# A router's ranking from one table of differences, its masks merged, and the low rows rounded by ScalarE and TensorE

## The reference

```python
u_inner = u @ W_in.T + b_in;  x, z = split(u_inner)
dbc = x @ W_x.T + b_x                      # delta_raw, B, C
delta = softplus(delta_raw @ W_dt.T + b_dt)
h_t = h_{t-1} * exp(delta_t * A) + x_t * delta_t * B_t ;  y_t = sum_n h_t C_t
y = (y + x * D) * silu(z) ; x = x + y @ W_out.T + b_out

logits = xn @ Wg.T + bg ; scores = softmax(logits)        # 4 experts
topv, topi = top_k(scores, 2)
base = xn @ Wi.T ; low = xn @ A[e].T (4 ranks for each expert)
out = sum over the 2 chosen e of score_e * (relu(base + low_e @ B_e.T) @ Wo.T)
```

## Time and profile before

| | |
|---|---|
| median of 3 runs | 1856.04 us (1853.64 to 1858.43) |
| profiled execution | 1855.82 us, of which span 1854.0 us |
| granted TensorE clock, mean of the span | 0.959 of full speed |
| VectorE busy | 1763.7 us (95% of the span), 2060 instructions |
| GpSimd busy | 1714.5 us (92%) |
| TensorE busy | 1624.7 us (88%) |
| ScalarE busy | 1503.9 us (81%) |

### The profile page before, as it was taken

One profiled execution on the slowest core, in us unless ns is written; L12 is line 12 of the kernel. 1 busy time (PEld: TensorE's weight loads), 2 busy tenths in 40 slices (PEclk: granted clock), 3 DMA queues, 4 the chain that ended last, 5 costly groups with the idle time before them and its releaser, 6 DMA issues.

```text
span 1854.0 us, 26281 instructions
## 1 busy us (share of the span) xinstructions
PE 1624.7 (88%) x7052; PEld 830.2 (45%) x7052; DVE 1763.7 (95%) x2060; ACT 1503.9 (81%) x3113; POOL 1714.5 (92%) x649
## 2 busy tenths in 40 slices
PE   6657689998998999889898989989899998988999
PEld 3213244444444444444444444444444444444465
DVE  5999999999999999999999999999999999999951
ACT  4776889888898988889898888979888897988643
POOL 1999999999999999999999999999999999999910
PEclk9767799999999999999999999999999999999999
DMA  6655565655656565554747556574665657475200
GB/s 211 138 137 139 118 154 140 157 129 138 152 107 174 131 166 128 141 141 108 181 116 170 140 129 146 111 185 118 165 143 127 137 118 190 99 167 136 63 7 18
DMA packets 150070, 249.07 MB, mean 134 GB/s; under 512 B 22432, under 2 KB 47264, under 8 KB 149408
## 3 DMA queue, kind: packets, MB, share of 16 engines
q1 hardware_dynamic: 145456, 231.09, 51.0%
q0 software_dynamic: 4464, 16.25, 4.6%
HBM read 188.01 MB, written 42.99 MB: 125 GB/s over the span
## 4 chain that ended last, share of the span: by engine, by line
DVE 35%; PE 18%; issue 17%; POOL 16%; ACT 7%; DMA 2%; SPq 1%; DVEq 0%; POOLq 0%; ACTq 0%
DVE decay L1395 15%; POOL hs L1470 10%; DVE hs L1382 9%; DVE hs L1395 7%; POOL hs L1482 4%; PE bank L914 3%; PE bank L962 3%; ACT decay L1203 3%; PE y_ps L998 2%; PE bank L984 2%; POOL z_dt L1450 2%; PE bank L918 1%; DMA b_rep<-bc_scratch 1%; DVE silu L1282 1%; PE bank L979 1%
## 5 line engine op out<-in xcount | busy, mean ns | idle before, releaser
L1470 POOL TENSOR_TENSOR hs<-dx_rep,b_rep 128x2048 f32<-128x2048 f32 x255 | 1188.9, 4678 | 43.1 <-DVE hs L1411 40.0
L1395 DVE TENSOR_TENSOR_SCAN decay<-decay,state,hs 128x512 f32<-128x512 f32 x640 | 791.5, 1270 | 4.9 <-ACT decay L1203 3.9
L1203 ACT ACTIVATE decay<-dt_rep,a_sb 128x512 f32<-128x512 f32 x1024 | 692.5, 685 | 20.6 <-DVE dx_rep L1409 1.8
L1395 DVE TENSOR_TENSOR_SCAN hs<-decay,state,hs 128x512 f32<-128x512 f32 x384 | 485.8, 1265 | 1.3 <-ACT decay L1203 0.8
L1482 POOL TENSOR_TENSOR hs<-hs,c_rep 128x1024 f32<-128x1024 f32 x192 | 476.5, 2482 | 6.0 <-ACT state L1217 5.8
L1382 DVE TENSOR_TENSOR hs<-decay,c_rep 128x1024 f32<-128x1024 f32 x320 | 383.7, 1199 | 0.0
L998 PE MATMUL y_ps<-hs,nsum 128*32 128x512 f32 x2048 | 292.2, 645 | 53.5 <-POOL hs L1482 44.8
L914 PE MATMUL bank<-xn_t,w_in_sb 128*128 128x512 f32 x512 | 252.6, 622 | 10.3 <-DVE silu L1282 3.5
L962 PE MATMUL bank<-w_i_sb,x_t 128*128 128x512 f32 x492 | 249.6, 631 | 8.2 <-DVE silu L1282 6.9
L984 PE MATMUL bank<-w_o_sb,r_t 128*128 128x256 f32 x944 | 217.0, 383 | 4.7 <-ACT r_t L1186 2.7
L984 PEld LDWEIGHTS bank<-w_o_sb,r_t 128*128 128x128 f32 x944 | 178.8, 191 | 56.2 <-issue 28.5
(11 more groups left out here) (170 smaller groups left out, 1823.9 us busy)
## 6 DMA issues: line engine op xcount, KB each, us to landing
dx_rep<-rep_scratch SPq DMA_DIRECT2D x252, 256.0 KB, 4.7
dt_rep<-rep_scratch SPq DMA_DIRECT2D x252, 256.0 KB, 7.6
b_rep<-bc_scratch SPq DMA_DIRECT2D x256, 64.0 KB, 4.0
c_rep<-bc_scratch SPq DMA_DIRECT2D x256, 64.0 KB, 2.4
rep_scratch<-z_dt SPq DMA_DIRECT2D x64, 256.0 KB, 2.6
rep_scratch<-e_dt SPq DMA_DIRECT2D x64, 256.0 KB, 2.7
e_dt<-z_dt POOLq DMA_DIRECT2D x31, 512.0 KB, 4.6
xin<-in_u SPq DMA_DIRECT2D x16, 512.0 KB, 4.1
```

What stands on the lines that cost most here:

```text
L1203: nc.scalar.activation(decay[:, j, :], dt_rep[m % 2][:, j, :], ACT.Exp, scale=a_sb[:, J * s + j:J * s + j + 1]).then_inc(decay_ready, 1)
L1395: v.tensor_tensor_scan(hs[s % 4][:, j, :] if kept else decay[:, j, :], decay[:, j, :], hs[s % 4][:, j, :], state[:, b, n:n + 1], ALU.mult, ...
L1470: nc.gpsimd.tensor_tensor(hs[s % 4][:], dx_rep[m % 2][:], b_rep[:, k, :].unsqueeze(1).to_broadcast([P, J, T]), ALU.mult).then_inc(input_re ...
```

## The change

The routing takes seven parts instead of ten (`LAST_H` 6). One table `gap` holds all differences of logits, one `scalar_tensor_tensor` makes from it and `tri` the table of "stands ahead of" with ties settled, and its sum is the rank. One instruction makes both masks `sel` (rank 0 and rank 1), and one multiplies both into the low rows. The second copy of the logits, the tables, the rank and the masked rows no longer lie in PSUM: `lg`, `gap`, `gt`, `rank`, `sel` and `low` are SBUF tiles. The two writes of `pk` leave VectorE: ScalarE spreads `low` into `pk` four times (a new job H0 of ScalarE), and rounding and rest are made behind the transposes: ScalarE rounds the transposed rows into `low_t` (I0), TensorE subtracts from the same bank what was rounded, by a product with `neg_low` (I1), and ScalarE writes `low_t` again (I1). The tables of all engines are moved a little around that.

```diff
 DVE_SIDE
     "H3 post | H4 post | H5 post | H6 post",
-    "K2 late, H7 post | H8 post | H9 post | M0 post",
+    "K2 late |  |  | M0 post",
 ACT_SIDE
-    " | J7 late, S7 late | T6 late, X0 post | T7 late",
-    " | I0 post | E3 main | V3 main",
+    " | J7 late, S7 late | T6 late, X0 post, H0 post | T7 late",
+    " | I0 post, I1 post | E3 main | V3 main",
 ...
 # TensorE
+                if letter == "I" and i == 1:
+                    pe.wait_ge(low_hi, q + 1)
+                    pe.matmul(banks[used("I0", c, AHEAD[when])[0]][:], neg_low[:], low_t[:], start=False, stop=True,
+                              skip_group_check=True).then_inc(low_rest, 1)
+                    return
 ...
 # ScalarE
+                elif letter == "H":
+                    act.wait_ge(low_ready, q + 1)
+                    nc.scalar.copy(pk[:].rearrange("p t a b w -> p (t a) b w"),
+                                   low[:].rearrange("p t a w -> p (t a) w").unsqueeze(2).to_broadcast([P, 2 * TT, 4, NE * LR])
+                                   ).then_inc(freed[used("H0", c, AHEAD[when])[0]], 1)
+                elif letter == "I" and i == 1:
+                    act.wait_ge(low_rest, q + 1)
+                    b, _ = used("I0", c, AHEAD[when])
+                    nc.scalar.activation(low_t[:], banks[b][:], ACT.Identity).then_inc(freed[b], 1)
 ...
 # VectorE, route
                 if i == 0:
                     dve.wait_ge(filled[b], count)
-                    v.tensor_tensor(lg[:], z[:, :, 0:NE], b_g_sb[:], ALU.add)
-                    last = v.tensor_tensor(lgp, z[:, :, 0:NE], b_g_sb[:], ALU.add)
+                    last = v.tensor_tensor(lg[:], z[:, :, 0:NE], b_g_sb[:], ALU.add)
 ...
                     v.tensor_reduce(mx[:], lg[:], AX, ALU.max)
-                    v.tensor_tensor(gtp, lgp.unsqueeze(2).to_broadcast([P, TT, NE, NE]),
-                                    lg[:].unsqueeze(3).to_broadcast([P, TT, NE, NE]), ALU.is_gt)
-                    last = v.tensor_tensor(eqp, lgp.unsqueeze(2).to_broadcast([P, TT, NE, NE]),
-                                           lg[:].unsqueeze(3).to_broadcast([P, TT, NE, NE]), ALU.is_equal)
+                    last = v.tensor_tensor(gap[:], lg[:].unsqueeze(2).to_broadcast(grid), lg[:].unsqueeze(3).to_broadcast(grid),
+                                           ALU.subtract)
                 elif i == 2:
-                    v.tensor_tensor(lm[:, :, 0:NE], lgp, mx[:].unsqueeze(2).to_broadcast([P, TT, NE]), ALU.subtract)
-                    last = v.tensor_tensor(eq[:], eqp, tri[:], ALU.mult)
+                    v.tensor_tensor(lm[:, :, 0:NE], lg[:], mx[:].unsqueeze(2).to_broadcast([P, TT, NE]), ALU.subtract)
+                    last = v.scalar_tensor_tensor(out=gt[:], in0=tri[:], scalar=-TINY, in1=gap[:], op0=ALU.mult, op1=ALU.is_lt)
                 elif i == 3:
-                    last = v.tensor_tensor(gt[:], gtp, eq[:], ALU.add)
+                    last = v.tensor_reduce(rank[:], gt[:].rearrange("p t e f -> p (t e) f"), AX, ALU.add)
                 elif i == 4:
-                    last = v.tensor_reduce(rank, gt[:], AX, ALU.add)
+                    last = v.tensor_tensor(sel[:, 0::2], rank[:].unsqueeze(1).to_broadcast([P, 2, TT * NE]),
+                                           ranks[:].unsqueeze(2).to_broadcast([P, 2, TT * NE]), ALU.is_equal)
                 elif i == 5:
-                    for a in range(2):
-                        last = v.tensor_scalar(sel[:, a], rank, float(a), None, ALU.is_equal)
+                    v.tensor_tensor(own2[:], lm[:, :, 0:NE], sel[:, 2].rearrange("p (t e) -> p t e", t=TT), ALU.mult)
+                    last = v.tensor_tensor(sel[:, 1], sel[:, 2], sel[:, 0], ALU.subtract)
                 elif i == 6:
+                    v.tensor_reduce(lm[:, :, NE], own2[:], AX, ALU.add).then_inc(router, 1)
+                    shape = [P, 2, TT, NE, LR]
+                    last = v.tensor_tensor(
+                        low[:].rearrange("p t a (e r) -> p a t e r", e=NE),
+                        z[:, :, NE:].rearrange("p t (e r) -> p t e r", e=NE).unsqueeze(1).to_broadcast(shape),
+                        sel[:, 0:2].rearrange("p a (t e) -> p a t e", t=TT).unsqueeze(4).to_broadcast(shape), ALU.mult)
```

More of the change, by code:

```diff
@@ L42 @@
 BOUND = 41.0
+TINY = 1.1754944e-38
 PE_SIDE = [
@@ L415, in bank_jobs @@
                     name = {"Y": "F", "Z": "J"}.get(name[0], name[0]) + name[1]
-                if name[0] in BANK_JOBS and name != "C1":
+                if name[0] in BANK_JOBS and name not in ("C1", "I1"):
                     yield name, when, J * s + j
@@ L571, in block_program @@
         gt = sb("gt", [P, TT, NE, NE])
-        eq = sb("eq", [P, TT, NE, NE])
-        sel = sb("sel", [P, 2, TT, NE])
-        change = sb("change", [P, TT, NE])
+        gap = sb("gap", [P, TT, NE, NE])
+        rank = sb("rank", [P, TT * NE])
+        ranks = sb("ranks", [P, 2])
+        sel = sb("sel", [P, 3, TT * NE])
         own2 = sb("own2", [P, TT, NE])
         wgt = [sb(f"wgt{i}", [P, 2, TT]) for i in range(2)]
-        pk = sb("pk", [P, TT, 2, 2, 2, NE * LR])
+        low = sb("low", [P, TT, 2, NE * LR])
+        pk = sb("pk", [P, TT, 2, 4, NE * LR])
         decay = ctx.enter_context(nc.psum_tensor("decay", [P, J, T], F32))
@@ L950, in job_pe @@
                     for t in range(TT):
-                        mm = pe.transpose(ps[:, t * P:(t + 1) * P], pk[:, t].rearrange("p a b c d -> p (a b c d)"), ident[:])
+                        mm = pe.matmul(ps[:, t * P:(t + 1) * P], pk[:, t].rearrange("p a b w -> p (a b w)"), ident[:],
+                                       start=t == 0, stop=False, is_transpose=True, skip_group_check=True)
                 elif letter in "ZJ":
@@ L1227, in _ @@
                 v.memset(consts[:, n], value)
+            for rank_of in range(2):
+                v.memset(ranks[:, rank_of:rank_of + 1], float(rank_of))
             v.memset(bound[:], BOUND).then_inc(zeroed, 1)
@@ L1313, in route @@
                 b, count = used("H0", c, AHEAD[when])
[L1314 to L1322, removed]
+                z = banks[b][:, 0:TT * (NE + NE * LR)].rearrange("p (t w) -> p t w", t=TT)
+                grid = [P, TT, NE, NE]
                 if i == 0:
                     dve.wait_ge(filled[b], count)
-                    v.tensor_tensor(lg[:], z[:, :, 0:NE], b_g_sb[:], ALU.add)
-                    last = v.tensor_tensor(lgp, z[:, :, 0:NE], b_g_sb[:], ALU.add)
+                    last = v.tensor_tensor(lg[:], z[:, :, 0:NE], b_g_sb[:], ALU.add)
                 else:
@@ L1345, in route @@
+                    last = v.tensor_tensor(sel[:, 1], sel[:, 2], sel[:, 0], ALU.subtract)
                 elif i == 6:
-                    v.tensor_tensor(own2[:], lgp, sel[:, 1], ALU.mult)
-                    v.scalar_tensor_tensor(out=change[:], in0=rank, scalar=1.0, in1=sel[:, 0], op0=ALU.is_equal,
-                                           op1=ALU.subtract)
-                    last = v.tensor_tensor(msk[:, :, 0], low, sel[:, 0].unsqueeze(3).to_broadcast([P, TT, NE, LR]), ALU.mult)
-                elif i == 7:
-                    v.tensor_reduce(second, own2[:], AX, ALU.add)
-                    last = v.tensor_tensor(msk[:, :, 1], low, change[:].unsqueeze(3).to_broadcast([P, TT, NE, LR]), ALU.mult)
-                elif i >= 8:
-                    flat = ps[:, 256:384].rearrange("p (t w) -> p t w", w=NE * LR)
-                    both = [P, 2 * TT, 2, NE * LR]
-                    parts_ = pk[:].rearrange("p t a b c w -> p (t a) b c w")
-                    if i == 8:
-                        v.tensor_tensor(lm[:, :, NE], second, mx[:], ALU.subtract).then_inc(router, 1)
-                        last = v.tensor_copy(parts_[:, :, :, 0].bitcast(F32R), flat.unsqueeze(2).to_broadcast(both))
-                    else:
-                        last = v.tensor_tensor(parts_[:, :, :, 1], flat.unsqueeze(2).to_broadcast(both), parts_[:, :, :, 0],
-                                               ALU.subtract)
@@ L1365, in weigh_choices @@
+                last.then_inc(low_ready if i == LAST_H else mask_step, 1)
             def weigh_choices(i, q, odd):
@@ L1418, in body @@
                         v.tensor_scalar(neg_id[:], ident[:], -1.0, None, ALU.mult)
+                        for part in range(2):
+                            v.tensor_scalar(neg_low[:].rearrange("p (x c w) -> p x c w", x=4, c=2)[:, :, part],
+                                            ident[:].rearrange("p (x c w) -> p x c w", x=4, c=2)[:, :, part], -float(part), None,
+                                            ALU.mult)
                         split_weights(w_dt_st, hs[1][:, 0, :], 1)
```

35 lines of the change are left out of this document (19 added, 16 removed), and 43 rows, old and new, of tables (ACT_END, ACT_LAST, ACT_SIDE, DVE_SIDE).

## The result

The changed kernel takes 1999.96 us (median of 4 runs: 1970.06, 1998.73, 2001.19, 2002.29) against 1855.11 us before, 1.078 times as long. The two longest runs count as slow, since they lie more than 1.5% above the shortest, so the ratio on record, 1.069 with a 95% interval of 1.065 to 1.073, rests on 1970.06 and 1998.73 alone. The profiled execution took 1998.73 us, of which 1996.9 us are span, 142.9 us more than the span before. The prediction of 1997 us is met by three of the four executions; what the total is made of was predicted less well.

A forecast was written before the change was run, and what follows sets the result against it. VectorE's list was taken to bound the 108.35 us chunk, GpSimd having 0.5 us of slack. Stalls less the 1.2 us won, 9.4 x 15 = 141 us on 1855.8, gave 1997 us; range 1849 to 2045, exclusion's own 1950 to 2045.

The forecast's parts named there:

- What bounds the kernel: Middle chunk of 108.35 us: as long as VectorE's list, with GpSimd at 107.8 us and some 0.5 us of slack.
- What the change takes from VectorE: Routing: VectorE's small instructions and `pk` writes fall from 2.31 to 1.11 us, 1.2 us per chunk.
- Exclusion: Six routing instructions with two SBUF operands each wait until GpSimd's running instruction is over; 1997 us, chance 0.68.
- The size of the stalls: Six routing instructions: 8.2 to 15.2 us of waits per routing, 7.5 to 13.8 after allowing for GpSimd's idling.
- idle in a tenth of the chunk: GpSimd, in the longer chunk: runs dry of scans while VectorE stands, idle about a tenth of the time.
- The chunk, forecast at 115 to 121 us: Sign of being right: a middle chunk lasts 115 to 121 us instead of 108.35.
- ScalarE's wait between I0 and I1: ScalarE waits some 2 us for TensorE in each chunk; up to 30 us if uncovered, put at nothing.
- The tail of the program: Last turn: TensorE's chain gets one product longer, 0.3 us with the setup of the tables.
- No exclusion: Rival: SBUF operands cost nothing, GpSimd becomes the bound; 7 us won, 1849 us, chance 0.16.
- Partial hold: Rival: VectorE and GpSimd share in short turns, 1.2 us a chunk, 1874 us; chance 0.05 together with a ScalarE stall.

The follow-up runs named there:

- the first experiment: The changed kernel, but each of the six two-operand routing instructions keeps one operand in PSUM: 1855.82 us against 1856.14 before, ratio 0.9991.
- the last experiment: The first experiment's kernel without job I1 (TensorE's product with `neg_low`, ScalarE's second write of `low_t`): 1853.99 us, ratio to before 0.9992.
- `gap` alone: The first experiment's kernel, but `gap` reads two SBUF tensors again: 1886.47, 1902.84, 1930.70 and 1932.21 us.

## Why the prediction was right, point by point

*What bounds the kernel.* Right, shown by the first and the last experiment: 1.0 us per chunk taken from VectorE gives 0.46 in a short chunk, and taking VectorE's wait away too gives nothing more on average. GpSimd's slots summed to 107.8 us, a short chunk of the first experiment is 107.94. The sum is no hard floor: in the last experiment chunks of 107.4 and 108.9 us take turns.

*What the change takes from VectorE*, 1.2 us per chunk. Nearly right: the first experiment, with two small instructions more, is busy for 1750.3 us instead of 1763.7, 0.84 us per chunk where the slots gave 1.04.

*Exclusion.* Right, and shown: 1999.96 us with the operands in SBUF, 1855.82 with one of each pair in PSUM, a probe that costs 0.06 us or 1.5 with the place of one operand alone changed, waits that end where a GpSimd instruction ends, and none in the last routing, where GpSimd stands. The rule of the Trainium skill ("SBUF — State Buffer", Who interferes with whom) agrees as far as which instructions collide: two SBUF inputs of VectorE against a GpSimd that reads SBUF. That the second waits until the other is over agrees too (`gap` 4.5 us behind a large product). The runs add that a waiting VectorE can be passed over.

*The size of the stalls.* 7.5 to 13.8 us per routing were given and 10.6 taken (9.4 plus the 1.2 won). Measured against the same forms in the first experiment: gap 3680 - 220 ns, lm 1883 - 162, gt 351 - 207, sel 1247 - 173, own 1635 - 156, the difference 905 - 160, together 8.6 us for each of the 16 routings, 138 us in all, 9.2 per routing beside a busy GpSimd. The sum nearly stands; its terms don't. A mean wait of 1.8 us assumed random phases. The phase is locked: `gap` came right behind the start of the large product in twelve of the 15 and cost 4.4 us, `lm` 1.5 where 2.8 was written, and the last four were free in nine of the 15, since GpSimd then stood for ScalarE's logarithm. In five routings one of them waited 7.4 to 12 us, which no term had. That GpSimd would be idle in a tenth of the chunk was about right (6 of 114 us in the cheap chunk, 19 of 127 in the dear one), but it was idle just where the stalls would have been. The chunk, forecast at 115 to 121 us, lasted 118.6 on average.

*ScalarE's wait between I0 and I1, put at nothing.* It costs no time where GpSimd is the clock (the last experiment), but the reason given, that decays come ahead of time all through the chunk, is wrong: the scan behind I1 waits 0.44 us for its decay in the first experiment and 0.64 in the changed kernel (at 1073.38). There GpSimd isn't the clock, and VectorE's idle time counts: 6.0 and 15.8 us ahead of its scans instead of 4.9 and 1.3, some 16 us that were not in the sum. Two thirds of them come without any stall, for the first experiment has 8.8 and 8.3. The tail of the program, put at 0.3 us, is longer too: from the last routing to the end 52.2 us before, 53.1 in the first experiment, 54.8 in the changed kernel.

*Why 1997 is so close.* Partly by luck: errors cancelled. The stalls were 21 us less than was taken (138 against 10.6 x 15 = 159). VectorE's idle time rose by 19.3 us, put at nothing. What is left of the rise of its busy time, 138 - 123.6, is 14.4 us won, where 18 were taken. So 138 - 14.4 + 19.3 = 142.9 us against 141. The execution of 1970.06 us, 27 us off, shows that the hit could as well have missed by that much.

*The rivals.* No exclusion: ruled out. Its 1849 us would have been too hopeful by some 7 us even without stalls (1855.82 in the first experiment): a few longer chunks ate what the short ones gave. Partial hold: ruled out by 4.4 us waits that end on GpSimd's ends.

*Still open.* Why VectorE is let in at some ends and not at others. What is shown is that moving the DMA issue took away the waits of 12 us, and that most of the ends passed over have a long overlap, with the two of 0.06 us against it. That GpSimd's next instruction is then already queued is a reading, not tested. Open is also what sets the phase: the times of single executions differ by 1.6% in the changed kernel and by 2.4% with `gap` alone, under 0.5% before.

## What to carry to other kernels

Where VectorE and GpSimd both work all the time, let no instruction of VectorE in that stretch read two SBUF tensors, nor scale one from SBUF to SBUF, however small it is (a plain copy was not tried; a reduction did not stall): a PSUM copy of one operand costs 0.08 us, a stall 1.5 on average and up to 12. Such a stall is printed as duration: look for a small shape with a large mean. And do not sum up stalls one by one. They move to the next instruction of the kind, and with fewer instructions at risk the kernel was in two cases slower than with all six; with none it was back at its old time.

## What the runs showed of the hardware

- A `tensor_scalar` of VectorE on 16 elements from SBUF to SBUF stalls beside a busy GpSimd like one with two SBUF operands: median 1.04 us, at most 11.4, against 0.14 for a `tensor_tensor` with a PSUM operand. A `tensor_reduce` of 64 elements from SBUF to SBUF does not (at most 0.22 us).
- A VectorE instruction that waits for GpSimd can be passed over by two further GpSimd instructions: 12 us in fourteen of the sixteen routings of one kernel, behind a DMA issue of GpSimd, and 7.9 us once in another, ahead of it.
- The wait does not depend on the size: 16 and 64 elements both wait out a product of 4.5 us.
